# A routed feed-forward layer on one core: group 2's weights loaded later, logits' parts added on TensorE, counts by choice, tables in five parts, one subtraction moved ahead

## The chip, the cores and the metric

One core of a Trainium2 chip runs one program. The metric is the device time of one execution, in microseconds (us). The kernel before takes 1415.31 us, the median of 3 runs (1414.93 to 1415.47).

## What is computed

The reference adds to x (4 x 1024 rows of 512 floats) a mixture-of-experts layer applied to a rotated x. Cut to what matters:

```python
rot = hamilton(q_left_n, hamilton(filtered(x), q_right_conj))  # 4x4 mix of the 4 quarters of a row
logits = rot @ gate_w.T                     # 4096 tokens x 8 experts
topv, topi = top_k(softmax(logits), 2)      # first and second choice of each token
gates = topv / sum(topv)
for j in range(2):                          # place of each token in its expert's list
    mask = one_hot(topi[:, j], 8)
    loc_j = cumsum(mask) - 1 + offset       # all first choices stand before the second ones
    offset += mask.sum(0)
valid = loc < 1024                          # 1024 slots for each expert
h = relu(disp @ fc1_w.T + fc1_b)            # 8 experts, 1024 slots, 512 -> 2048
eo = h @ fc2_w + fc2_b                      # 2048 -> 512
out = x + sum_over_choices(eo[slot] * gate * valid)
```

## The kernel before

Tokens lie as 128 partitions x 32 (token = 32 p + j). The five engines run programs written out by hand, tied by semaphores, with no planner: the order of the source lines of an engine is the order of its work. There are three stages.

**Routing.** x comes in eight chunks of 4 tiles (512 tokens). For each of 32 units (chunk, quarter of the row) TensorE makes four 128x128 transposes (line 1171), ScalarE takes the high part (518), VectorE the low part (796), and TensorE, three units behind, multiplies both with the rotated gate weights, 16 columns: 8 for the high and 8 for the low part of those weights (1151, 1152). After four units ScalarE copies the 16 x 512 sums into `logitsT` (512), and `turn_logits` (1154 to 1160) turns them with four transposes into 128 x 16 pieces of a PSUM bank: seven times within the loop, and once after it. VectorE then adds the two parts into `lg` with one reduction (817), and chooses twice: `reduce_max`, equality, product, `reduce_max`, equality (821 to 825), with the first choice masked out of `score` (827) in between. `hot` holds the one-hot masks of both choices.

One scan over 512 columns counts both choices at once (831). TensorE turns the last counts of each partition into starting numbers (1188, 1189: sums over the partitions before, and for the second choice all first choices too). VectorE adds them, masks with `hot`, and reduces to a place for each token (838 to 840). Then come the tables: for each choice and half of j (JH = 16 tiles), in four parts, VectorE makes `hot_t` (861), `hot_b` (863) and `hot_q` (865), ScalarE the second half of `hot_q` (538), and TensorE multiplies the two with 16 matmuls a part (1203) into `token_ps`: the token of each slot. Line 868 subtracts the first low parts of group 0's weights before VectorE waits for these matmuls (`hots_used`); 870 to 872 make `gather_row`, by which GpSimd gathers the first eight blocks of rows (392), one indirect DMA for each. `idle` (1194) keeps TensorE busy with products that nobody reads.

**The first slab.** TensorE turns the gathered rows (1212), and VectorE rotates them (`rotate_ps` 949 to 959, 12 instructions a call; `rotate_half` 961 to 972) upon first terms that ScalarE wrote (569). TensorE makes one quarter itself (1219). VectorE's order is written out at 989 to 1007:

```python
turn_w1(1); sum_w1(1, 0); sum_w1(1, 1); sum_w1(1, 2)
rotate_ps(0)
w1_low_parts(1, 0)
rotate_ps(1); rotate_half(2)
y_low(0, B11, y11); y_low(0, B21, y21)
rotate_half(3)
```

`w1_low_parts(1, 0)` (786) makes the first low parts of group 1's weights; it waits for ScalarE's high parts (502) alone. Sums of the rotated halves follow (909, 913, 916), and TensorE goes on at 1296.

**The experts.** 8 experts, each with two slabs of 512 slots, a Strassen-like scheme of seven products for fc1 in `product` (1228 to 1230, three matmuls for a float32 product) and `fc2` (1253 to 1263). Weights of fc1 come in groups of two tiles.

**SP's queue.** It loads x, group 0's weights `load_w1(0)`, copies x to the output (309), then has `load_w1(1)`, `load_w1(2)`, `cut_x(0)` and `cut_x(1)` in this order (310 to 313). `load_w1` issues 8 DMAs of 64 KB, and waits for VectorE's transpose of the group before (286), since the buffer `w1_raw` has room for one group. `cut_x` waits for rows that GpSimd gathered and stored (298). Group 2's weights are first used by `turn_and_sum(2)` (1043), and `turn_x(0)` (1075) is the first user of `cut_x(0)`; it stands behind that line.

Of the kernel before, what the change touches and what calls it, by code (L numbers as in the profile page):

```python
# [11 lines left out]
ALU = mybir.AluOpType  # L12
# [6 lines left out]
def program(nc, x, cond, q_right, spectral, gate_w, fc1_w, fc1_b, fc2_w, fc2_b, out):  # L19
# [19 lines left out]
    JH = TJ // 2  # L39
    BLK = 32  # L40
# [35 lines left out]
    with ctx:  # L76
# [46 lines left out]
        lg = sb("lg", [P, TJ, E], where=early)  # L123
# [62 lines left out]
        logits_hl = xp_all.rearrange("p (j a e) -> p j a e", a=2, e=E)  # L186
        ahead_ps = hp[:, 0, 0:TOPK * E]
# [80 lines left out]
        def _(sp):  # L268
# [41 lines left out]
            load_w1(1)  # L310
            load_w1(2)
# [27 lines left out]
        def _(pool):  # L339
            chain = [0]  # L340

            def link(ins):
# [6 lines left out]
                               pattern=[[-1, P]], channel_multiplier=1).then_inc(consts_ready, 1)  # L349
            link(pool.memset(sign[:, :, :, :], 1.0))  # L350
# [29 lines left out]
            pool.wait_ge(counts_ready, 1)  # L380
# [112 lines left out]
        def _(act):  # L493
# [41 lines left out]
            for c in range(2 * TOPK):  # L535
                k, pairs = c // 2, slice(c % 2 * JH // 2, (c % 2 + 1) * JH // 2)
                act.wait_ge(hot_t_ready, c + 1)
                act.activation(hot_q[:, k, pairs, 1, :, :], hot_t[:, c % 2, :, :, :], ACT.Copy, scale=part_f[:, :]
                               ).then_inc(hots_p_ready, 1)
# [177 lines left out]
        def _(dve):  # L717
# [97 lines left out]
            hot3 = hot[:, :, :, :].rearrange("p k e j -> p (k e) j")  # L815
            dve.wait_ge(logits_T, CHUNKS)
            link(dve.tensor_reduce(lg[:, :, :], logits_hl.rearrange("p j a e -> p j e a"), X, ALU.add))
            first_bc = first_f[:, :].unsqueeze(1).to_broadcast([P, TJ, E])
            for k, (v, w, from_) in enumerate(((mx, w1m, lg[:, :, :]), (v2, w2m, score[:, :, :]))):
# [6 lines left out]
                if k == 0:  # L826
                    dve.scalar_tensor_tensor(score[:, :, :], hot_k, -1e30, lg[:, :, :], ALU.mult, ALU.add).then_inc(masked, 1)
                    dve.wait_ge(masked, 1)

            dve.wait_ge(consts_ready, 3)  # L830
            dve.tensor_tensor_scan(cnt[:, :, :].rearrange("p k j -> p (k j)"),
                                   carry[:, :, :].rearrange("p k j -> p (k j)"),
                                   hot[:, :, :, :].rearrange("p k e j -> p (k e j)"), 0.0, ALU.mult, ALU.add
                                   ).then_inc(counts_ready, 1)
# [14 lines left out]
            def of_pairs(ap, width):  # L849

                return ap.rearrange("p (m t) -> p m t", t=2).unsqueeze(2).to_broadcast([P, JH // 2, width, 2])

            for c in range(2 * TOPK):
                k, js = c // 2, slice(c % 2 * JH, (c % 2 + 1) * JH)
                pairs = slice(c % 2 * JH // 2, (c % 2 + 1) * JH // 2)
                numbers = value[:, :, :].unsqueeze(1).to_broadcast([P, JH // 2, P, 2])
# [3 lines left out]
                blocks = spaced[:, :, :].unsqueeze(1).to_broadcast([P, JH // 2, BLOCKS, 2])  # L860
                dve.tensor_tensor(hot_t[:, c % 2, :, :, :], blocks, of_pairs(q_f[:, k, js], BLOCKS),
                                  ALU.is_equal).then_inc(hot_t_ready, 1)
                dve.tensor_tensor(hot_b[:, k, pairs, :, :], numbers, of_pairs(b_f[:, k, js], P), ALU.is_equal)
                dve.wait_ge(hot_t_ready, c + 1)
                dve.tensor_tensor(hot_q[:, k, pairs, 0, :, :], hot_t[:, c % 2, :, :, :], of_pairs(j1[:, js], BLOCKS),
                                  ALU.mult).then_inc(hots_ready, 1)

            w1_low_parts(0, 0)
            dve.wait_ge(hots_used, 2 * TOPK)
# [122 lines left out]
            sum_w1(1, 2)  # L992
            rotate_ps(0)
            w1_low_parts(1, 0)
# [133 lines left out]
        def _(pe):  # L1128
# [70 lines left out]
            for c in range(2 * TOPK):  # L1199
                pe.wait_ge(hots_ready, c + 1)  # L1200
                pe.wait_ge(hots_p_ready, c + 1)
                for j in range(c % 2 * JH, (c % 2 + 1) * JH):
                    ins = pe.matmul(token_ps, hot_b[:, c // 2, j // 2, :, j % 2], hot_q[:, c // 2, j // 2, :, :, j % 2],
                                    start=(c == 0 and j == 0), stop=(c == 2 * TOPK - 1 and j == TJ - 1))
# [200 lines left out]
```

## Time and profile before

| what | value |
|---|---|
| median of 3 runs | 1415.31 us (1414.93 to 1415.47) |
| the profiled execution, its own time | 1415.69 us |
| span of that execution in the trace | 1413.7 us |
| TensorE busy in the span | 1378.0 us (97%) |
| VectorE / ScalarE / GpSimd busy | 1053.3 / 705.0 / 314.6 us |
| mean granted TensorE clock | 0.99 of full speed |

Engines are PE (TensorE matmul), PEld (TensorE weight load, beside PE), DVE (VectorE), ACT (ScalarE), POOL (GpSimd), SP (its DMA queue). A row of a timeline has the start in us, the time from the first start to the last end, the engine, the line, the operation with written and read tiles, shapes, and in brackets how long the engine stood idle before it and what ended that. "x4" is four instructions merged into one row. In the chain of waits each row is a step of the chain that ended last, with its start and the time that it adds. A busy engine says little by itself: what counts is the wait that ends last at each step.

### The profile page before, as it was taken

The numbers are of one execution on the slowest core, as the hardware profiler recorded it, in microseconds if no ns is written. First come the engines' busy times: TensorE is split into PE (matmuls) and PEld (weight loads), VectorE is DVE, ScalarE is ACT, GpSimd is POOL, SyncE is SP. The second block draws the span as 40 slices with busy tenths as digits, with TensorE's granted clock in tenths as the row PEclk, the third lists the DMA queues.
The fourth block names the chain that finished last, engine by engine and source line by source line (L and its number), as shares of the span: only waits on it lengthen the run. The fifth ranks groups of instructions, "written<-read, shape, count | busy, mean of one in ns | idle before, by whom it ended". The sixth has DMA issues, their size and how long they took to land.

```text
span 1413.7 us, 18054 instructions
## 1 busy us (share of the span) xinstructions
PE 1378.0 (97%) x6175; PEld 1131.0 (80%) x6175; DVE 1053.3 (75%) x1582; ACT 705.0 (50%) x1058; POOL 314.6 (22%) x333
## 2 busy tenths in 40 slices
PE   8679999999999999999999999999999999999997
PEld 6458888888888888888888888888888888888885
DVE  6898779687877778687886878687796868865443
ACT  5456455544555445455464455454455454644442
POOL 1174203320125103221034202241032200220021
PEclk9799999999999999999999999999999999999998
DMA  8677666656457555566466565575465533543232
GB/s 286 252 175 180 131 129 178 156 115 140 106 164 172 133 99 157 150 133 146 88 187 164 106 136 133 144 162 137 90 179 148 110 75 67 156 119 69 52 104 74
DMA packets 449676, 194.41 MB, mean 138 GB/s; under 512 B 398464, under 2 KB 401673, under 8 KB 447794
## 3 DMA queue, kind: packets, MB, share of 16 engines
q1 hardware_dynamic: 427378, 125.98, 40.5%
q0 software_dynamic: 22208, 67.29, 15.3%
q8 instruction: 49, 0.80, 0.2%
q14 instruction: 41, 0.34, 0.1%
HBM read 153.47 MB, written 39.98 MB: 137 GB/s over the span
## 4 chain that ended last, share of the span: by engine, by line
PE 95%; DVE 3%; DMA 1%; issue 1%; ACT 0%; SPq 0%; POOL 0%; POOLq 0%
PE ps L1253 15%; PE ps L1257 15%; PE ps L1263 15%; PE ps L1228 14%; PE ps L1229 14%; PE ps L1230 14%; PE ps L1171 1%; PE ps L1244 1%; PE ps L1245 1%; PE ps L1246 1%; DVE yfull L958 1%; PE ps L1151 1%; PE ps L1152 1%; DMA x_all<-in_x 0%; DVE yfull L971 0%
## 5 line engine op out<-in xcount | busy, mean ns | idle before, releaser
L1228 PE MATMUL ps<-yc_hi,w1c_hi 128*128 128x512 f32 x896 | 349.5, 390 | 1.2 <-DVE yc_lo L924 1.2
L1230 PE MATMUL ps<-yc_hi,w1c_lo 128*128 128x512 f32 x896 | 348.7, 389 | 0.0
L1229 PE MATMUL ps<-yc_lo,w1c_hi 128*128 128x512 f32 x896 | 348.6, 389 | 0.0
L1253 PE MATMUL ps<-w_hi,h_hi 128*128 128x512 f32 x952 | 254.4, 389 | 0.0
L1257 PE MATMUL ps<-w_hi,h_lo 128*128 128x512 f32 x952 | 254.4, 389 | 0.0
L1263 PE MATMUL ps<-w_lo,h_hi 128*128 128x512 f32 x952 | 254.4, 389 | 0.0
L1263 PEld LDWEIGHTS ps<-w_lo,h_hi 128*128 128x128 f32 x952 | 178.7, 188 | 37.2
L1253 PEld LDWEIGHTS ps<-w_hi,h_hi 128*128 128x128 f32 x952 | 178.7, 188 | 37.1
L1257 PEld LDWEIGHTS ps<-w_hi,h_lo 128*128 128x128 f32 x952 | 178.7, 188 | 37.0
L1228 PEld LDWEIGHTS ps<-yc_hi,w1c_hi 128*128 128x128 f32 x896 | 168.1, 188 | 39.2 <-DVE yc_lo L924 2.2
L1230 PEld LDWEIGHTS ps<-yc_hi,w1c_lo 128*128 128x128 f32 x896 | 168.2, 188 | 35.3
L1229 PEld LDWEIGHTS ps<-yc_lo,w1c_hi 128*128 128x128 f32 x896 | 168.2, 188 | 34.4
L897 DVE TENSOR_TENSOR w_lo<-w_raw,w_hi 128x512 fp32r<-128x512 f32 x232 | 158.3, 683 | 0.4 <-ACT w_hi L554 0.4
L891 DVE TENSOR_TENSOR w1c_lo<-w1t,w1c_hi 128x1792 fp32r<-128x1792 f32 x62 | 125.6, 2026 | 31.5 <-ACT w1c_hi L547 31.5
L692 ACT ACTIVATE h_hi<-h 128x512 fp32r<-128x512 f32 x128 | 80.9, 632 | 134.8 <-PE ps L1263 117.0
L554 ACT ACTIVATE w_hi<-w_raw 128x512 fp32r<-128x512 f32 x232 | 143.7, 620 | 0.4 <-DMA w_raw<-in_L_ffn_fc_w 0.4
L976 DVE SCALAR_TENSOR_TENSOR h_lo<-h,h_hi 128x512 fp32r<-128x512 f32 x128 | 88.4, 692 | 57.7 <-ACT h_hi L692 56.6
L547 ACT ACTIVATE w1c_hi<-w1t 128x1792 fp32r<-128x1792 f32 x62 | 105.8, 1706 | 44.7 <-DVE w1t L781 44.7
L976 DVE SCALAR_TENSOR_TENSOR h_lo<-ps,h_hi 128x512 fp32r<-128x512 f32 x64 | 44.0, 688 | 106.3 <-ACT h_hi L598 106.3
L1013 DVE SCALAR_TENSOR_TENSOR h<-ps,b1T,s 128x512 f32<-128x512 f32 x64 | 47.8, 747 | 91.2 <-PE ps L1230 91.1
L946 DVE SCALAR_TENSOR_TENSOR yfull<-x_turned,rot,yfull 128x512 f32<-128x512 f32 x168 | 114.8, 746 | 0.0
L654 ACT ACTIVATE s<-ps 128x512 f32<-128x512 f32 x64 | 38.3, 598 | 142.7 <-PE ps L1230 142.7
(182 smaller groups left out, 1506.4 us busy)
## 6 DMA issues: line engine op xcount, KB each, us to landing
w_raw<-in_L_ffn_fc_w SPq DMA_DIRECT2D x232, 256.0 KB, 3.0
w_raw<-in_L_ffn_fc_w SPq DMA_DIRECT2D x512, 64.0 KB
slots_dram<-x_blk POOLq DMA_DIRECT2D x28, 512.0 KB, 3.8
x_blk<-slots_dram SPq DMA_DIRECT2D x224, 64.0 KB, 2.6
out<-x_all SPq DMA_DIRECT2D x8, 1024.0 KB, 13.0
x_all<-in_x SPq DMA_DIRECT2D x6, 1024.0 KB, 13.7
b_bc<-in_L_ffn_fc_b POOLq DMA_DIRECT2D x8, 256.0 KB, 3.8
x_all<-in_x SPq DMA_DIRECT2D x4, 256.0 KB, 3.8
```

What stands on the lines that cost most here:

```text
L547: act.activation(w1c_hi[:, G % 2, :, :], w1t[:, 1:8, :], ACT.Copy).then_inc(w1_hi_ready, 1)
L554: act.activation(w2_hi[:, v % 3, :], w2_raw[:, v % 3, :], ACT.Copy).then_inc(w2_hi_ready, 1)
L891: dve.tensor_tensor(w1c_lo[:, G % 2, :, :], w1t[:, 1:8, :], w1c_hi[:, G % 2, :, :].bitcast(F32), ALU.subtract).then_inc(w1_ready, 1)
L897: dve.tensor_tensor(w2_lo[:, v % 3, :], w2_raw[:, v % 3, :], w2_hi[:, v % 3, :].bitcast(F32), ALU.subtract).then_inc(w2_ready, 1)
L946: ins = dve.scalar_tensor_tensor(y, x_turned[:, :, j, :], rot[:, i, j:j + 1], y, ALU.mult, ALU.add)
L976: dve.scalar_tensor_tensor(h_lo[:, N % 3, :], full, 0.0, h_hi[:, N % 3, :].bitcast(F32), ALU.max, ALU.subtract).then_inc(h_ready, 1)
L1228: pe.matmul(bank, hi, yc_hi[:, y, q, :], start=first and q == 0, stop=False, skip_group_check=True)
L1229: pe.matmul(bank, hi, yc_lo[:, y, q, :], start=False, stop=False, skip_group_check=True)
L1230: ins = pe.matmul(bank, lo, yc_hi[:, y, q, :], start=False, stop=last and q == 1, skip_group_check=True)
L1253: pe.matmul(eo_s[:, b, :], h_hi[:, c, blk], w2_hi[:, w, :], start=False, stop=False, skip_group_check=True)
L1257: pe.matmul(eo_s[:, b, :], h_lo[:, c, blk], w2_hi[:, w, :], start=False, stop=False, skip_group_check=True)
L1263: ins = pe.matmul(eo_s[:, b, :], h_hi[:, c, blk], w2_lo[:, w, :], start=False, stop=False, skip_group_check=True)
```

## The change

It makes five edits, all in the first 112 us of the program. `load_w1(2)` now waits, on SP's queue, for the eight gathers of the first slab. `turn_logits` multiplies by a 16 x 8 matrix `both_parts` (two identities, one above the other) in place of transposing, so that both parts are added on TensorE and the reduction into `lg` is gone; the choices read PSUM. The counts are scanned for each choice by itself, and TensorE's starting numbers come in two steps. The tables are made in five parts in place of four, the last two of 8 tiles. `w1_low_parts(1, 0)` stands before `rotate_ps(0)`.

```diff
+    PARTS = ((0, 0, JH), (0, JH, TJ), (1, 0, JH), (1, JH, TJ - JH // 2), (1, TJ - JH // 2, TJ))
-        lg = sb("lg", [P, TJ, E], where=early)
+        both_parts = sb("both_parts", [2 * E, E], where=early)
-        logits_hl = xp_all.rearrange("p (j a e) -> p j a e", a=2, e=E)
-        ahead_ps = hp[:, 0, 0:TOPK * E]
+        logits_ps = xp_all[:, 0:TJ * E].rearrange("p (j e) -> p j e", e=E)
+        ahead_ps = [hp[:, k, 0:E] for k in range(TOPK)]
...
             load_w1(1)
+
+            for arrived in x0_in:
+                sp.wait_ge(arrived, 16)
             load_w1(2)
...
+            pool.wait_ge(consts_ready, 1)
+            pool.tensor_tensor(both_parts[:, :], ident[0:2 * E, 0:E], ident[0:2 * E, E:2 * E], ALU.add)
...
-            pool.wait_ge(counts_ready, 1)
+            pool.wait_ge(counts_ready, 2)
...
-            for c in range(2 * TOPK):
-                k, pairs = c // 2, slice(c % 2 * JH // 2, (c % 2 + 1) * JH // 2)
+            for c, (k, begin, end) in enumerate(PARTS):
                 act.wait_ge(hot_t_ready, c + 1)
...
             dve.wait_ge(logits_T, CHUNKS)
-            link(dve.tensor_reduce(lg[:, :, :], logits_hl.rearrange("p j a e -> p j e a"), X, ALU.add))
-            for k, (v, w, from_) in enumerate(((mx, w1m, lg[:, :, :]), (v2, w2m, score[:, :, :]))):
+            for k, (v, w, from_) in enumerate(((mx, w1m, logits_ps), (v2, w2m, score[:, :, :]))):
...
-            dve.wait_ge(consts_ready, 3)
-            dve.tensor_tensor_scan(cnt[:, :, :].rearrange("p k j -> p (k j)"),
+                    dve.wait_ge(consts_ready, 3)
+                dve.tensor_tensor_scan(cnt[:, k * E:(k + 1) * E, :].rearrange("p e j -> p (e j)"),
...
-            dve.wait_ge(ahead_ready, 1)
-            link(dve.tensor_tensor(cnt[:, :, :], cnt[:, :, :], ahead_ps.unsqueeze(2).to_broadcast([P, TOPK * E, TJ]), ALU.add))
-            link(dve.tensor_tensor(loc[:, :, :], cnt[:, :, :], hot3, ALU.mult))
+            for k in range(TOPK):
+                of_k = slice(k * E, (k + 1) * E)
+                dve.wait_ge(ahead_ready, k + 1)
+                link(dve.tensor_tensor(cnt[:, of_k, :], cnt[:, of_k, :], ahead_ps[k].unsqueeze(2).to_broadcast([P, E, TJ]), ALU.add))
+                ins = dve.tensor_tensor(loc[:, of_k, :], cnt[:, of_k, :], hot[:, k, :, :], ALU.mult)
+            link(ins)
...
-            for c in range(2 * TOPK):
-                k, js = c // 2, slice(c % 2 * JH, (c % 2 + 1) * JH)
-                pairs = slice(c % 2 * JH // 2, (c % 2 + 1) * JH // 2)
+            for c, (k, begin, end) in enumerate(PARTS):
+                js, pairs, m = slice(begin, end), slice(begin // 2, end // 2), (end - begin) // 2
...
             w1_low_parts(0, 0)
-            dve.wait_ge(hots_used, 2 * TOPK)
+            dve.wait_ge(hots_used, len(PARTS))
...
             sum_w1(1, 2)
+            w1_low_parts(1, 0)
             rotate_ps(0)
-            w1_low_parts(1, 0)
             rotate_ps(1)
...
-                    at = (g * XC + t) * 2 * E
-                    ins = pe.transpose(xp_all[:, at:at + 2 * E], logitsT[:, g % 2, t * P:(t + 1) * P],
-                                       ident[0:2 * E, 0:2 * E])
+                    at = (g * XC + t) * E
+                    ins = pe.matmul(xp_all[:, at:at + E], logitsT[:, g % 2, t * P:(t + 1) * P], both_parts[:, :],
+                                    start=True, stop=True)
...
             pe.wait_ge(counts_ready, 1)
-            pe.matmul(ahead_ps, before[:, :], cnt[:, :, TJ - 1], start=True, stop=False)
-            pe.matmul(ahead_ps[:, E:2 * E], ones[:, :], cnt[:, 0:E, TJ - 1], start=False, stop=True).then_inc(ahead_ready, 1)
+            pe.matmul(ahead_ps[1], ones[:, :], cnt[:, 0:E, TJ - 1], start=True, stop=False)
+            pe.matmul(ahead_ps[0], before[:, :], cnt[:, 0:E, TJ - 1], start=True, stop=True).then_inc(ahead_ready, 1)
+            pe.wait_ge(counts_ready, 2)
+            pe.matmul(ahead_ps[1], before[:, :], cnt[:, E:2 * E, TJ - 1], start=False, stop=True).then_inc(ahead_ready, 1)
...
-            for c in range(2 * TOPK):
+            for c, (k, begin, end) in enumerate(PARTS):
                 pe.wait_ge(hots_ready, c + 1)
                 pe.wait_ge(hots_p_ready, c + 1)
-                for j in range(c % 2 * JH, (c % 2 + 1) * JH):
+                for j in range(begin, end):
```

## Rows read from the trace of the kernel before

**Rows 1.** The page's first line.

```profile
span 1413.7 us, 18054 instructions
```

**Rows 2.** The chain of waits, 26 to 31 us: start, us, what.

```profile
26.48 0.35 PE ps L1158 x4
...
30.58 0.35 PE ps L1158 x4
```

**Rows 3.** Table by stretch: stretch, length, each engine's busy us, PEclk, DMA share, GB/s.

```profile
14.00:42.00 28.00, 28.00 (x189) 19.20 (x188) 20.88 (x36) 18.69 (x34) 0.00 (x0) 1.00 0.96 339
44.00:57.00 13.00, 5.50 (x15) 4.39 (x16) 11.26 (x23) 5.43 (x14) 3.55 (x7) 0.53 1.02 380
...
66.00:68.00 2.00, 2.00 (x17) 1.90 (x16) 0.85 (x3) 0.00 (x0) 0.00 (x0) 0.50 0.00 0
```

**Rows 4.** TensorE: two rows of the timeline; line 1219's loads, ns min/median/max.

```profile
51.76 0.58 PE L1188 MATMUL ps<-cnt,before 128*128 128x16 f32 x2 [7.50 <-DVE cnt L831]
52.17 0.57 PE L1189 MATMUL ps<-cnt,ones 128*128 128x8 f32 x2
...
L1219 PEld LDWEIGHTS ps<-x_turned,rows x32: 190/190/192, 85.3 to 91.8; 128*128 128x128 f32 x32
```

**Rows 5.** Timeline of VectorE, from the logits to the places.

```profile
44.03 0.69 DVE L817 TENSOR_REDUCE lg<-ps 128x256 f32<-128x512 f32 x1 [2.06 <-PE ps L1158]
...
45.22 0.42 DVE L822 TENSOR_TENSOR s<-lg,st 128x256 f32<-128x256 f32 x1
...
50.38 1.23 DVE L831 TENSOR_TENSOR_SCAN cnt<-carry,s 128x512 f32<-128x512 f32 x1
...
52.78 0.69 DVE L838 TENSOR_TENSOR cnt<-cnt,ps 128x512 f32<-128x512 f32 x1 [1.09 <-PE ps L1189]
...
53.51 0.69 DVE L839 TENSOR_TENSOR loc<-cnt,s 128x512 f32<-128x512 f32 x1
...
54.23 1.05 DVE L840 TENSOR_REDUCE place<-loc 128x64 f32<-128x512 f32 x1
```

**Rows 6.** Timeline of the tables' last part, VectorE and TensorE.

```profile
63.20 0.68 DVE L861 TENSOR_TENSOR hot_t<-spaced,q_f 128x1024 bf16<-128x1024 bf16 x1
...
63.80 1.21 DVE L863 TENSOR_TENSOR hot_b<-value,b_f 128x2048 bf16<-128x2048 bf16 x1
...
64.93 0.68 DVE L865 TENSOR_TENSOR hot_q<-hot_t,j 128x1024 bf16<-128x1024 bf16 x1
...
65.53 0.94 DVE L786 TENSOR_TENSOR w1c_lo<-w1t,w1c_hi 128x768 fp32r<-128x768 f32 x1
65.67 1.89 PE L1203 MATMUL ps<-hot_q,hot_b 128*128 128x128 bf16 x16 [1.25 <-DVE hot_q L865]
...
67.59 0.22 DVE L870 COPY j_part<-ps 128x64 f32<-128x64 f32 x1 [1.11 <-PE ps L1203]
```

**Rows 7.** Timeline of the first gathers and the first rotations.

```profile
70.37 1.52 POOL L392 DMA_INDIRECT h<-in_x,gather_row  x1 [0.30 <-issue]
...
71.86 7.01 SPq L256 DMA_DIRECT2D w_raw<-in_L_ffn_fc_w  x8
...
72.50 0.66 PE L1212 MATMUL ps<-ident,h 128*128 128x128 f32 x4 [1.81 <-DMA h<-in_x,gather_row]
...
74.55 0.66 PE L1212 MATMUL ps<-ident,h 128*128 128x128 f32 x4 [0.71 <-DMA h<-in_x,gather_row]
...
75.75 5.05 DVE L958 SCALAR_TENSOR_TENSOR yfull<-ps,rot,yfull 128x256 f32<-128x256 f32 x12 [1.74 <-ACT yfull L569]
...
80.72 0.95 DVE L786 TENSOR_TENSOR w1c_lo<-w1t,w1c_hi 128x768 fp32r<-128x768 f32 x1
```

**Rows 8.** Timeline of SP's queue, TensorE and VectorE behind the first rotations.

```profile
89.94 14.30 SPq L256 DMA_DIRECT2D x_blk<-slots_dram  x16
...
97.94 0.93 PE L1296 MATMUL ps<-yc_hi,w1c_hi 128*128 128x512 f32 x3 [1.16 <-DVE yfull L916]
...
111.02 1.30 DVE L768 STREAM_TRANSPOSE w1t<-w_raw 128x512 f32<-128x512 f32 x2
```

More of the change, by code:

```diff
@@ L534, in _ @@
             act.wait_ge(part_ready, 1)
-            for c in range(2 * TOPK):
-                k, pairs = c // 2, slice(c % 2 * JH // 2, (c % 2 + 1) * JH // 2)
+            for c, (k, begin, end) in enumerate(PARTS):
                 act.wait_ge(hot_t_ready, c + 1)
-                act.activation(hot_q[:, k, pairs, 1, :, :], hot_t[:, c % 2, :, :, :], ACT.Copy, scale=part_f[:, :]
+                act.activation(hot_q[:, k, begin // 2:end // 2, 1, :, :], hot_t[:, c % 2, 0:(end - begin) // 2, :, :], ACT.Copy,
+                               scale=part_f[:, :]
                                ).then_inc(hots_p_ready, 1)
@@ L847, in _, with of_pairs @@
             link(dve.scalar_tensor_tensor(b_f[:, :, :], block_f[:, :, :], -float(P), place[:, :, :], ALU.mult, ALU.add))
-            def of_pairs(ap, width):
-                return ap.rearrange("p (m t) -> p m t", t=2).unsqueeze(2).to_broadcast([P, JH // 2, width, 2])
-            for c in range(2 * TOPK):
-                k, js = c // 2, slice(c % 2 * JH, (c % 2 + 1) * JH)
-                pairs = slice(c % 2 * JH // 2, (c % 2 + 1) * JH // 2)
-                numbers = value[:, :, :].unsqueeze(1).to_broadcast([P, JH // 2, P, 2])
+            for c, (k, begin, end) in enumerate(PARTS):
+                js, pairs, m = slice(begin, end), slice(begin // 2, end // 2), (end - begin) // 2
+                def of_pairs(ap, width):
+                    return ap.rearrange("p (m t) -> p m t", t=2).unsqueeze(2).to_broadcast([P, m, width, 2])
+                numbers = value[:, :, :].unsqueeze(1).to_broadcast([P, m, P, 2])
+                blocks = spaced[:, :, :].unsqueeze(1).to_broadcast([P, m, BLOCKS, 2])
+                table = hot_t[:, c % 2, 0:m, :, :]
                 if c >= 2:
@@ L859, in _ @@
                     dve.wait_ge(hots_ready, c - 1)
-                blocks = spaced[:, :, :].unsqueeze(1).to_broadcast([P, JH // 2, BLOCKS, 2])
-                dve.tensor_tensor(hot_t[:, c % 2, :, :, :], blocks, of_pairs(q_f[:, k, js], BLOCKS),
-                                  ALU.is_equal).then_inc(hot_t_ready, 1)
+                dve.tensor_tensor(table, blocks, of_pairs(q_f[:, k, js], BLOCKS), ALU.is_equal).then_inc(hot_t_ready, 1)
                 dve.tensor_tensor(hot_b[:, k, pairs, :, :], numbers, of_pairs(b_f[:, k, js], P), ALU.is_equal)
                 dve.wait_ge(hot_t_ready, c + 1)
-                dve.tensor_tensor(hot_q[:, k, pairs, 0, :, :], hot_t[:, c % 2, :, :, :], of_pairs(j1[:, js], BLOCKS),
-                                  ALU.mult).then_inc(hots_ready, 1)
+                dve.tensor_tensor(hot_q[:, k, pairs, 0, :, :], table, of_pairs(j1[:, js], BLOCKS), ALU.mult
+                                  ).then_inc(hots_ready, 1)
             w1_low_parts(0, 0)
-            dve.wait_ge(hots_used, 2 * TOPK)
+            dve.wait_ge(hots_used, len(PARTS))
             link(dve.tensor_copy(j_part[:, :], token_ps[:, 0, :]))
@@ L1198, in _ @@
             idle(12)
-            for c in range(2 * TOPK):
+            for c, (k, begin, end) in enumerate(PARTS):
                 pe.wait_ge(hots_ready, c + 1)
                 pe.wait_ge(hots_p_ready, c + 1)
-                for j in range(c % 2 * JH, (c % 2 + 1) * JH):
-                    ins = pe.matmul(token_ps, hot_b[:, c // 2, j // 2, :, j % 2], hot_q[:, c // 2, j // 2, :, :, j % 2],
-                                    start=(c == 0 and j == 0), stop=(c == 2 * TOPK - 1 and j == TJ - 1))
+                for j in range(begin, end):
+                    ins = pe.matmul(token_ps, hot_b[:, k, j // 2, :, j % 2], hot_q[:, k, j // 2, :, :, j % 2],
+                                    start=(c == 0 and j == 0), stop=(c == len(PARTS) - 1 and j == TJ - 1))
                 ins.then_inc(hots_used, 1)
```

9 lines of the change are left out of this document (4 added, 5 removed).

## The prediction

> **What bounds the kernel now.** I read the chain of waits first. The span is 1413.7 us [rows 1], and from about 110 us on every step of the chain is a TensorE matmul behind another: the experts run back to back. The change touches nothing there, so what it does to the start is passed on whole to the end. In the start the chain has four stretches.
>
> From 14 to 42 us it stays on TensorE. A turn of logits stands in it with 0.35 us for four transposes, and the next one follows 4.10 us later, like all seven of the loop [rows 2]. In the table by stretch TensorE is busy for 28.00 of 28.00 us at full clock, VectorE for 20.88 and ScalarE for 18.69 [rows 3]: there is no gap in which more TensorE work could hide. From 44 to 65.6 us VectorE holds the chain (choices, counts, tables), with one wait of 1.09 us for TensorE in between [rows 5], and a tail behind the last table [rows 6]. Then come the gathers; the second one ends VectorE's idle 1.74 us [rows 7]. From 75.75 on VectorE works without a stop until 97.8 us, where TensorE takes over after having waited 1.16 us for it [rows 8].
>
> The sum is made against the profiled execution: 1415.69 us, 2.0 over its span [rows 1], and 0.38 over the median of the runs. A difference counts for both alike.
>
> **Logits' parts on TensorE.** Four transposes become four float32 matmuls. The trace records each float32 matmul that is not a transpose as two pairs of weight load and matmul: the one instruction of line 1188 is x2, the one of 1189 too, and between their first starts lie 52.17 - 51.76 = 0.41 us, so 0.205 us a pair [rows 4]. That was at a clock of 0.53 [rows 3], nearly half speed, and neither 16 nor 8 columns mattered; so the weight load sets it, and at full clock I take 0.103 us. A turn is then 8 x 0.103 = 0.83 us, against 0.35: +0.48. Seven in the loop and one behind it, all on the chain: **+3.84**. Both ends: if the pairs follow as closely as the transposes of the same tile, 0.35 / 4 = 0.0875 us [rows 2], it is 8 x 0.35 = +2.8; if each pair pays its whole weight load of 0.190 us at full clock [rows 4], unhidden, it is 8 x (1.52 - 0.35) = +9.4. I stay with 0.103, the same kind of instruction.
>
> The Trainium skill (TensorE: Matmul & The Clock Gate, section LDWEIGHTS) says that a weight load takes its columns over 1.2 in ns, however many rows are used. For 128 columns that is an estimate of 107 ns a pair, 0.86 us a turn: +0.51 for each turn where I take +0.48, and +0.24 on the sum. The trace does not bear the rule out for transposes, which cost 87.5 ns here with 16 rows [rows 2].
>
> In return the reduction at line 817 goes, 44.03 to 44.76 with its gap: **-0.73** [rows 5]. The maximum, the equality and the masking of the first choice now read PSUM. I price that at nothing: 512 columns take 0.69 us with a PSUM operand (838) and without one (839) [rows 5]. The Trainium skill (VectorE: DVE Perf Modes, section on the TRN2 errata) charges 120 in place of 58 cycles for a PSUM source, an estimate of 0.065 us for each of three instructions, +0.19 on the sum; the same two rows speak against it.
>
> The sum of two identities on GpSimd stands before the signs, about 1.5 us into the program, over 10 us before its first reader. It costs nothing unless VectorE should come to wait for the signs, and then a few tenths at most.
>
> **Counts by choice.** The scan of 1.23 us is cut in two. A second VectorE instruction adds its fixed part: 256 columns take 0.42 and 512 take 0.69 [rows 5], so 0.15 us is fixed, of which about half overlaps the neighbour: +0.08. Behind the scan (end 51.61) the places' reduction now starts at 54.23, 2.62 us later. Afterwards TensorE has one matmul to make after the second scan, 0.58 us [rows 4] with 0.15 before and 0.04 behind, so it is ready 0.77 us after the scan. Meanwhile VectorE adds and masks the first choice: small work to +0.12, two linked instructions of 256 columns at 0.45 to +0.99; the second choice starts at about +0.93 and needs two more, so the reduction starts at +1.83. That is -0.79, with the extra scan **-0.71**. Ends: -0.4, if the first choice's work does not fit into the wait, and -0.8. Nothing else waits at `counts_ready` 2: GpSimd's next result is needed some 15 us later.
>
> **Tables in five parts.** From the rows, 1024 elements take 0.60 us of VectorE's time and 2048 take 1.13 (63.20, 63.80, 64.93): 0.53 for each 1024, 0.07 fixed [rows 6]. One part more is three instructions more, +0.21. Gained is the tail: now the last table ends at 65.61, 16 matmuls run until 67.56 at a clock of 0.50 [rows 3], and line 870 starts 1.98 us behind the table [rows 6]. With 8 matmuls left, half of 1.89, line 870 could start at 0.05 + 0.95 + 0.03 = 1.03 us behind it; VectorE's own subtraction (0.94, begun 0.08 before the end) holds it to no less than 0.89. So -0.95 + 0.21 = **-0.74**. Ends: -0.3 if the slow clock reaches the part before the last too, so that the last one queues, and -0.88 at full clock.
>
> **Group 2's loads behind the gathers.** Now they start at 71.86, in the midst of the gathers. The first gather was issued by 70.07 and had its transposes at 72.50, 2.43 us; the second by 71.89 and 74.55, 2.66 us [rows 7]. With no loads beside it I give the second the first one's time: **-0.23** (ends 0 and -0.4). The later gathers gain more, but VectorE does not wait for them. Price: SP's queue now waits for the eighth gather, about 85 us, issues 8 DMAs in 7.01 us [rows 7] until 92, and only then the cuts, which start at 89.94 and take 14.30 us now [rows 8]; they end by 106.3 in place of 104.2. Group 2's weights are first read at 111.02 [rows 8], and the cuts behind that. Both covers hold, by some 15 and at least 5 us; were the first gone, each us of lateness would cost one.
>
> **Low parts ahead.** At 80.72 the subtraction takes 0.95 us of VectorE, 0.86 of it in the chain. Placed before the rotations it starts at 74.01, where VectorE idles until 75.75 [rows 7]; it ends by 74.96, before the rotations can start (75.5). **-0.86**. End: nothing, if VectorE's chain were not the last to arrive; excluded by the 1.16 us of [rows 8].
>
> **Sum:** 3.84 - 0.73 - 0.71 - 0.74 - 0.23 - 0.86 = +0.57 us: 1415.69 becomes 1416.26, and the median 1415.31 becomes 1415.9.
>
> A measurement of this kernel can tell about 0.2% from no change, 2.8 us. Forecast: **within it**, slightly on the slow side.
>
> **Rivals.**
> *The second pairs are free* (chance 0.10). If the second pair of each matmul ran under the first's shadow, the +3.84 goes, and the rest is 0.57 - 3.84 = -3.27: 1412.0, faster by 0.23%. For it: 8 columns are next to no streaming. Against it: the even spacing of 0.205 us at lines 1188 and 1189.
>
> *Weight loads stand open* (0.12, with what else may turn slower). In the loop other matmuls cover the weight loads; small matmuls have nothing to cover them with. At 0.190 us a pair the turn is 1.52 us, the sum -3.27 + 9.4 = +6.1: 1421.4. It becomes slower than 0.2% once a pair takes over (0.35 + 6.1 / 8) / 8 = 0.14 us at full clock. For it: a load is recorded with 0.190. Against it: lines 1188 and 1189 again, whose spacing at half clock is already only 0.205.
> The Trainium skill (FP8 and Floating Point Precision, section TensorE Precision Notes) counts four passes for true float32; if each of them loaded weights, a turn would be 16 x 0.103 = 1.65 us and the time 1422.4, in this rival too, but the trace records two loads.
>
> *The moved loads bring nothing* (inside the forecast, 0.2 of its chance): the second gather's time is its own latency, and the sum is +0.80: 1416.1.
>
> **How the numbers follow.** The forecast has 0.78. Its own range: the lower ends together, 2.8 - 0.73 - 0.8 - 0.88 - 0.4 - 0.86 = -0.9; the weak ends, 3.84 - 0.73 - 0.4 - 0.3 - 0 - 0.86 = +1.55, and to +2.8 for pairs of up to 0.14 us. So 1414.4 to 1418.1. To hold 8 in 10 with both rivals aside I reach somewhat to each: 1413.4 to 1418.8. Faster 0.10, within 0.78, slower 0.12.
>
> **What would show it.** Line 1158 with two pairs for each matmul, a turn of 0.8 us in the chain, groups of units 4.6 us apart in place of 4.1, and the loop's end 3.4 us later. No `lg`. The reduction of places 1.8 us behind the second scan. The last table part 8 matmuls, line 870 about 1 us behind it. SP's loads of group 2 after 82 us, `w1c_lo` of line 786 in VectorE's idle time before the rotations, and rotations starting at once behind each other. TensorE's take-over (1296) about 0.6 us later than 97.94. Wrong it would be with a turn near 0.35 or over 1.1 us, with a loop that had slack after all, or with a stall past 106 us on group 2's weights.

## The result, and the profile after

| | kernel before | changed kernel |
|---|---|---|
| median of the runs, us | 1415.51 (1414.51 to 1417.07) | 1418.03 (1417.06 to 1421.34) |
| ratio, 95% interval | 1 | 1.0021 (1.0013 to 1.0029) |
| profiled execution, us | 1415.69 | 1417.70 |
| its span, us | 1413.7 | 1415.7 |

The change makes the kernel slower, by 2.5 us in the medians, where the prediction said 0.57. That is the edge of what it called "within 0.2%", and inside its range (1413.4 to 1418.8). A ratio of 1 lies outside the interval, so the slowdown is real, though small.

First the opening lines of the profile's page for the changed kernel; they answer to [rows 1].

```profile
span 1415.7 us, 18135 instructions
## 1 busy us (share of the span) xinstructions
PE 1384.5 (98%) x6209; PEld 1138.7 (80%) x6209; DVE 1053.1 (74%) x1587; ACT 705.8 (50%) x1059; POOL 309.9 (22%) x334
```

Next the chain of waits of the changed kernel, 16 to 31 us, against [rows 2].

```profile
16.65 0.98 PE ps L1165 x8
...
21.39 0.98 PE ps L1165 x8
...
26.13 0.98 PE ps L1165 x8
```

The four transposes with 0.35 us became eight pairs (x8: two for each of four matmuls) with 0.98 us, and a turn comes every 4.74 us in place of 4.10. So a turn costs 0.63 more where the prediction had 0.48, and a pair 0.12 us in place of 0.103. The weight loads themselves are recorded with 0.187 us (one line's instructions, line 1165), so neighbouring pairs overlap in part:

```profile
L1165 PEld LDWEIGHTS ps<-both_parts,logitsT x64: 181/187/187, 16.6 to 47.2; 16*128 16x128 f32 x64
```

VectorE's timeline of the changed kernel, from the first choice to the places, answers to [rows 5]. Line 826 is the maximum of each choice, 827 the equality behind it, 835 a scan, 844 and 845 add and mask the counts, 847 reduces to the places.

```profile
47.52 0.42 DVE L826 TENSOR_REDUCE st<-ps 128x32 f32<-128x256 f32 x1 [3.35 <-PE ps L1165]
47.98 0.42 DVE L827 TENSOR_TENSOR s<-ps,st 128x256 f32<-128x256 f32 x1
...
51.22 0.40 DVE L826 TENSOR_REDUCE st<-score 128x32 f32<-128x256 f32 x1
51.65 0.42 DVE L827 TENSOR_TENSOR s<-score,st 128x256 f32<-128x256 f32 x1
...
53.70 0.69 DVE L835 TENSOR_TENSOR_SCAN cnt<-carry,s 128x256 f32<-128x256 f32 x1
...
54.39 0.41 DVE L844 TENSOR_TENSOR cnt<-cnt,ps 128x256 f32<-128x256 f32 x1
54.83 0.44 DVE L845 TENSOR_TENSOR loc<-cnt,s 128x256 f32<-128x256 f32 x1
55.19 0.41 DVE L844 TENSOR_TENSOR cnt<-cnt,ps 128x256 f32<-128x256 f32 x1
55.63 0.46 DVE L845 TENSOR_TENSOR loc<-cnt,s 128x256 f32<-128x256 f32 x1
56.13 1.05 DVE L847 TENSOR_REDUCE place<-loc 128x64 f32<-128x512 f32 x1
```

The wait of 1.09 us for TensorE is gone. The second scan ends by 54.39, and the places' reduction begins 1.74 us later; the prediction said 1.8.

The timeline of the tables' last part, VectorE and TensorE, answers to [rows 6].

```profile
67.31 0.42 DVE L872 TENSOR_TENSOR hot_q<-hot_t,j 128x512 bf16<-128x512 bf16 x1
67.64 0.95 DVE L793 TENSOR_TENSOR w1c_lo<-w1t,w1c_hi 128x768 fp32r<-128x768 f32 x1
67.79 0.63 PE L1213 MATMUL ps<-hot_q,hot_b 128*128 128x128 bf16 x8 [0.53 <-DVE hot_q L872]
...
68.51 0.22 DVE L877 COPY j_part<-ps 128x64 f32<-128x64 f32 x1
```

Eight matmuls are left behind the last table, and line 877 (870 before) starts 0.78 us behind the table's end by the record (67.73), where it was 1.98: VectorE goes from its own subtraction into it with no wait.

Last the timeline of the gathered rows and the first rotations, against [rows 7] and [rows 8].

```profile
70.03 0.96 POOL L399 DMA_INDIRECT h<-in_x,gather_row  x1 [13.19 <-DVE gather_row L879]
73.51 1.11 PE L1222 MATMUL ps<-ident,h 128*128 128x128 f32 x4 [2.51 <-DMA h<-in_x,gather_row]
74.27 1.63 PE L1204 MATMUL ps<-w1c_hi 128*128 128x512 f32 x3
74.85 0.95 DVE L793 TENSOR_TENSOR w1c_lo<-w1t,w1c_hi 128x768 fp32r<-128x768 f32 x1
75.70 1.00 PE L1222 MATMUL ps<-ident,h 128*128 128x128 f32 x4
77.25 10.01 DVE L965 SCALAR_TENSOR_TENSOR yfull<-ps,rot,yfull 128x256 f32<-128x256 f32 x24 [1.45 <-ACT yfull L576]
87.17 2.74 DVE L978 SCALAR_TENSOR_TENSOR yfull<-x_turned,rot,yfull 128x256 f32<-128x256 f32 x6
...
83.03 5.77 SPq L258 DMA_DIRECT2D w_raw<-in_L_ffn_fc_w  x8
90.86 7.50 SPq L258 DMA_DIRECT2D x_blk<-slots_dram  x8
```

The low part now lies in VectorE's idle time, and the 24 rotations run without a break. SP's loads of group 2 start at 83.03; those weights are turned at 111.69 with no wait, so both covers held. But the transposes take 1.11 and 1.00 us where they took 0.66, and three idle matmuls 1.63 where they took 0.94. The table by stretch of the changed kernel says why (columns as in [rows 3]); the first of its rows is the loop of the logits.

```profile
14.00:48.00 34.00, 32.93 (x218) 23.64 (x215) 20.47 (x37) 19.80 (x36) 0.00 (x0) 1.00 0.98 363
...
72.00:78.00 6.00, 4.49 (x20) 3.88 (x21) 4.45 (x9) 2.10 (x5) 4.64 (x5) 0.72 0.65 176
```

From 72 to 78 us the granted clock was 0.72, with part of the stretch (73.1 to 76.5 us) at the lower of the two levels (1.2 of 2.4 GHz). It fell near the end of TensorE's wait of 2.51 us for the gathered rows; before, there was a wait as well (1.81 us), but the transposes there ran at full clock. So the second block's transposes began 5.67 us behind the first gather's issue; before it was 74.55 - 69.11 = 5.44.

### The profile page after: what moved, and what is told of

It is laid out like the page before. It is cut to its first block, busy times and chain, and to the rows that moved or that the text cites. A ratio compares the mean times of both kernels' runs of the same rounds, so it can differ in the third digit from the quotient of the medians.

```text
span 1415.7 us, 18135 instructions
## 1 busy us (share of the span) xinstructions
PE 1384.5 (98%) x6209; PEld 1138.7 (80%) x6209; DVE 1053.1 (74%) x1587; ACT 705.8 (50%) x1059; POOL 309.9 (22%) x334
## 4 chain that ended last, share of the span: by engine, by line
PE 94%; DVE 3%; DMA 1%; issue 1%; ACT 0%; SPq 0%; another core or an unknown queue 0%; POOL 0%; POOLq 0%; ACTq 0%
PE ps L1267 15%; PE ps L1263 15%; PE ps L1273 15%; PE ps L1238 14%; PE ps L1240 14%; PE ps L1239 14%; PE ps L1254 1%; PE ps L1255 1%; PE ps L1256 1%; PE ps L1178 1%; DVE yfull L965 1%; DMA x_all<-in_x 1%; PE ps L1165 1%; PE ps L1158 0%; PE ps L1159 0%
```

## The experiments

I compare executions by marks: when the same instruction starts, minus its start in the profiled execution of the kernel before (us, negative is earlier). A turn is one group of logits on TensorE, "take-over" is line 1296, "fc2" the first matmul of the second layer in group 0 (110.53 before) and in group 1 (118.69 before).

| | first turn | seventh turn | last turn | places | line 870 | rotations | take-over | fc2, group 0 | fc2, group 1 |
|---|---|---|---|---|---|---|---|---|---|
| changed kernel | -1.63 | +2.22 | +2.85 | +1.90 | +0.92 | +1.49 | +0.97 | +0.66 | +1.98 |
| e2, logits only | +0.10 | +3.95 | +4.58 | +4.50 | +4.31 | +4.66 | | +4.64 | +4.82 |
| e3, without logits | -1.43 | -0.45 | -0.44 | -1.31 | -2.04 | -1.83 | -2.43 | -2.63 | -1.20 |
| e4, longer idle | -0.09 | +3.75 | +4.39 | +3.44 | +2.46 | +2.15 | | +1.58 | +2.70 |
| e9, before again | -1.76 | +0.05 | +0.05 | +0.06 | +0.05 | -0.13 | -0.13 | -0.13 | +0.93 |
| e10, changed again | -1.73 | +2.11 | +2.75 | +1.80 | +1.17 | +1.39 | +0.88 | +0.59 | +1.65 |

**e1, the changed kernel again**, on the chip of e2 to e4.

> The changed kernel once more. In its first trace TensorE's fc2 stood 0.66 us later than before at 110.5 us, but two announcements of finished matmuls reached ScalarE 1.4 and 1.7 us late between 111 and 117 us, and the span came out 2.0 us longer. Theory A (a chance event of that execution): here no such late announcement, group 1 stays unbroken, and the profile's shift at fc2's first matmul (110.53 before) of 0.5 to 2 us is the shift at the end. Theory B (the change makes it, by what its later loads do to the DMA traffic): a wait of about 1 us before TensorE's group 1 shows again near 117 us. Time 1416.5 to 1418.5 by either; a turn of logits 0.98 us in the chain.

Measured: 1418.37 us, 1.0015 (1.0006 to 1.0024). The slowdown repeats, about 2.3 us by the medians.

**e2, the logits' edit alone**, made on the kernel before:

```diff
-                    at = (g * XC + t) * 2 * E
-                    ins = pe.transpose(xp_all[:, at:at + 2 * E], ..., ident[0:2 * E, 0:2 * E])
+                    at = (g * XC + t) * E
+                    ins = pe.matmul(xp_all[:, at:at + E], ..., both_parts[:, :], start=True, stop=True)
...
-            link(dve.tensor_reduce(lg[:, :, :], logits_hl.rearrange("p j a e -> p j e a"), X, ALU.add))
```

> The kernel before with the logits' parts added on TensorE and nothing else changed. Theory A: a turn costs 0.98 in place of 0.35 us, eight of them on the chain, +5.0, less 0.73 for the reduction: +4.3 us, 1419.8 against 1415.5. Rival (the loop has slack, the time comes from elsewhere): less than +1.5 us.

Measured: 1419.55 us, 1.0018 (1.0009 to 1.0027). The ratios given with the runs are those on record, with their intervals; they need not be the quotient of the two medians, which would be 1.0024 here. Its loop began almost where that of before did, and fc2 comes 4.64 us late: 8 x 0.63 = 5.04 for the turns, 0.73 back for the reduction, and 0.35 lost between line 870 and the rotations. The median says less than the trace: 1419.55 is 3.4 us above the 1416.12 of the kernel before that was timed beside it. e9 below shows one place where such a price can hide, but e3 shows a higher price for the same edit.

**e3, the change without the logits' edit**: the reverse of that diff, made on the changed kernel.

> The changed kernel with the four transposes and the reduction on VectorE put back; the other four edits stay. Theory A: the four edits bring -0.9 (counts) -1.0 (tables) -0.86 (low parts) and -0.2 to +0.6 (gathers, and TensorE's clock that falls before them), so -2.2 to -3.0 us against before: 1412.5 to 1413.3. Rival (the moved loads cost as much as the rest gains): within 1 us of before.

Measured: 1413.51 us, 0.998 (0.9971 to 0.9989). The other four parts together gain 2.6 us, and the logits' edit costs more than they bring: 1418.37 - 1413.51 = 4.9 us. So the same edit cost 3.4 us on the kernel before and 4.9 us on the other four parts; the price by turns, 5.04 - 0.73 = 4.3, lies between. This version beats both kernels, by 0.2%.

**e4, longer idle work**, to test whether the clock ahead of the rotations is what was lost:

```diff
-            idle(11)
+            idle(16)
```

> The changed kernel with 16 in place of 11 products that nobody reads ahead of the first gathered rows. In its trace TensorE's clock fell to 0.5 at 72.9 us, the first transposes took 1.11 in place of 0.66 us, the three idle products behind them 1.63 in place of 0.94, and the second block's transposes waited behind these. Theory A: the 5 products (1.1 us at full clock) close the idle time of 2.51 us before 73.5 far enough that the clock stays at full, and VectorE's rotations start 0.5 to 0.8 us earlier: 0.5 to 0.8 us less than e1. Rival (the gather's landing alone sets that start): no difference to e1.

Measured: 1418.61 us, 1.0019 (1.001 to 1.0028). The table by stretch and TensorE's timeline of e4:

```profile
74.00:78.00 4.00, 2.64 (x14) 1.75 (x14) 3.35 (x8) 1.45 (x3) 3.08 (x4) 1.00 0.67 176
...
74.98 0.66 PE L1222 MATMUL ps<-ident,h 128*128 128x128 f32 x4 [1.32 <-DMA h<-in_x,gather_row]
75.39 0.94 PE L1204 MATMUL ps<-w1c_hi 128*128 128x512 f32 x3
76.71 0.66 PE L1222 MATMUL ps<-ident,h 128*128 128x128 f32 x4 [0.38 <-DMA h<-in_x,gather_row]
```

TensorE waits 1.32 us in place of 2.51 for the first rows, the granted clock stays 1.00, the transposes take 0.66 again, and the rotations start 6.35 us behind the first gather's issue, against 7.22 in the changed kernel (6.86 in e1, 6.64 before). The clock did cost 0.5 us or more at this place. That is not seen in the median: 1418.61 beside e1's 1418.37 is no gain. The trace of e4 cannot settle it either, since its loop began late: the last turn stands 1.5 us behind that of the changed kernel.

**e5 to e8, one part alone on the kernel before**: counts by choice, tables in five parts, and the two moves.

```diff
-            dve.tensor_tensor_scan(cnt[:, :, :].rearrange(...), ...).then_inc(counts_ready, 1)
+                dve.tensor_tensor_scan(cnt[:, k * E:(k + 1) * E, :].rearrange(...), ...).then_inc(counts_ready, 1)
...
-            pe.matmul(ahead_ps, before[:, :], cnt[:, :, TJ - 1], start=True, stop=False)
-            pe.matmul(ahead_ps[:, E:2 * E], ones[:, :], cnt[:, 0:E, TJ - 1], start=False, stop=True).then_inc(ahead_ready, 1)
+            pe.matmul(ahead_ps[1], ones[:, :], cnt[:, 0:E, TJ - 1], start=True, stop=False)
+            pe.matmul(ahead_ps[0], before[:, :], cnt[:, 0:E, TJ - 1], start=True, stop=True).then_inc(ahead_ready, 1)
+            pe.wait_ge(counts_ready, 2)
+            pe.matmul(ahead_ps[1], before[:, :], cnt[:, E:2 * E, TJ - 1], start=False, stop=True).then_inc(ahead_ready, 1)
```

```diff
+    PARTS = ((0, 0, JH), (0, JH, TJ), (1, 0, JH), (1, JH, TJ - JH // 2), (1, TJ - JH // 2, TJ))
...
-            for c in range(2 * TOPK):
+            for c, (k, begin, end) in enumerate(PARTS):
```

```diff
             load_w1(1)
+            for arrived in x0_in:
+                sp.wait_ge(arrived, 16)
             load_w1(2)
...
+            w1_low_parts(1, 0)
             rotate_ps(0)
-            w1_low_parts(1, 0)
```

The first fence is e5, the second e6; of the third, the wait is e7 and the move of the low parts e8.

> The kernel before with the counts by choice alone. Theory A: the places' reduction starts 0.7 to 0.9 us earlier, less what GpSimd's subtraction, now beside a scan, takes from VectorE: -0.7 us. Rival (the scan for each choice costs as much as it hides): 0.

> The kernel before with the tables in five parts alone. Theory A: the last table ends 0.21 us later, the tail behind it falls from 1.98 to 0.9 or 1.05 us, so the first gather is issued 0.75 to 0.95 us earlier; if TensorE's clock falls before the first gathered rows as in the changed kernel, 0.3 to 0.6 us of it are given back: -0.3 to -0.9 us. Rival: TensorE's clock is slow in both of the last parts and the tail stays near 2 us: +0.2.

> The kernel before with group 2's loads behind the first gathers alone. Theory A: the second gather's rows come 0.2 to 0.3 us earlier and the later ones 2 to 3 us, of which VectorE's chain sees 0.2: -0.2 us, and no wait by TensorE between 110 and 120 us. Theory B (these loads, now beside gathers and cuts, make the late stretch that the changed kernel showed at 112 to 117 us): a wait of about 1 us by TensorE near 116 us, and +1 us.

> The kernel before with group 1's low parts ahead of the rotations alone. Theory A: the subtraction runs in VectorE's idle 1.74 us before the rotations, which start at 75.75 as before, and everything behind comes 0.86 us earlier: -0.86 us. Rival: it delays GpSimd's issue of the third and fourth gather by 0.6 us each, so that VectorE later waits for rows or for ScalarE: 0.

| | median us | ratio (95%) | stretch of its own, against before |
|---|---|---|---|
| e5 counts | 1414.43 | 0.9995 (0.9986 to 1.0004) | first choice to places -0.87 |
| e6 tables | 1414.61 | 1.0 (0.9991 to 1.0009) | first table to line 870: -0.64 (changed kernel -0.98) |
| e7 loads | 1415.94 | 1.0002 (0.9993 to 1.0011) | line 870 to the second block's transposes -0.26 |
| e8 low parts | 1414.41 | 0.9995 (0.9986 to 1.0004) | rotations to the second half -0.87, given back by fc2 |

No single part can be told from nothing by its timed runs: against 1415.27 for the kernel before, timed beside them, the medians are lower by 0.8 (e5), 0.7 (e6) and 0.9 us (e8) and higher by 0.7 (e7), and each interval holds 1. The marks inside the traces tell more. The low parts alone are the instructive one. VectorE's timeline of e8, and behind it two rows of TensorE's:

```profile
75.44 10.01 DVE L958 SCALAR_TENSOR_TENSOR yfull<-ps,rot,yfull 128x256 f32<-128x256 f32 x24 [0.73 <-ACT yfull L569]
85.36 2.71 DVE L971 SCALAR_TENSOR_TENSOR yfull<-x_turned,rot,yfull 128x256 f32<-128x256 f32 x6
88.98 2.36 DVE L924 TENSOR_TENSOR yc_lo<-yfull,yc_hi 128x1024 fp32r<-128x1024 f32 x2 [0.91 <-ACT yc_hi L619]
91.26 2.71 DVE L971 SCALAR_TENSOR_TENSOR yfull<-x_turned,rot,yfull 128x256 f32<-128x256 f32 x6
94.33 1.23 DVE L909 TENSOR_TENSOR x_turned<-ps,yfull 128x1024 f32<-128x1024 f32 x1 [0.37 <-PE ps L1219]
...
84.98 1.01 PE L1212 MATMUL ps<-ident,h 128*128 128x128 f32 x4 [0.27 <-DMA h<-in_x,gather_row]
85.79 8.43 PE L1219 MATMUL ps<-x_turned,rows 128*128 128x256 f32 x32
```

The rotations run back to back and are through 0.86 us sooner, and then VectorE waits 0.91 for ScalarE and 0.37 for TensorE, which have their input from the gathered rows. With group 2's loads still beside the gathers the last of those rows come no sooner than before: its transposes start at 84.98, before at 84.87. But the clock has a part in it: from 83 to 88 us the granted clock of e8 was 0.71, before 1.00. The last transposes took 1.01 us in place of 0.66, and the 32 matmuls of line 1219 8.43 in place of 7.07. So an estimate from these rows is that some 0.35 of the 0.91 us, and all of the 0.37, are the clock's, and 0.55 the rows'. In the changed kernel, where the loads are out of the way, the last transposes start at 82.93 and the same place has no such wait: 89.84 follows 87.17 + 2.74 at once.

This is one execution, and the profiled one of e8 took 1415.65 us where the median is 1414.41. That the low parts alone bring nothing is shown for this execution and not for e8's others.

**e9, the kernel before again, and e10, the changed kernel again**, on one chip, because the first profiles left two things open: seven turns cost 4.4 us and the changed kernel was only 2.85 us late at the start of the last one, since it had begun the loop 1.63 us earlier; and it lost another 1.3 us between the two fc2 marks, in group 1.

> The kernel before, profiled once more. Theory A (late announcements belong to a chip or an execution): its trace may show them, as the traces of the call with the changed kernel did and those of the single edits did not. Theory B (they belong to the change): never here. Besides, its first trace had a slow clock from 10.5 to 14.0 us; without it the loop is 1 to 1.5 us earlier, and fc2 begins near 109.3 in place of 110.53. Time 1415.5.

> The changed kernel a third time, beside the kernel before. Theory A: late announcements only if e9 has them too; without them the end is 2.2 to 2.6 us later than e9's, measured from the first turn of logits. Theory B: TensorE waits about 1 us near 117 us again. Time +2 to +3 us on before.

Measured: e9 1415.98 us, 0.9999 (0.9989 to 1.0008); e10 1418.26, 1.002 (1.0011 to 1.003). Both questions have their answer in e9. Its chain of waits, 30 to 36 us:

```profile
30.81 3.25 DMA w_raw<-in_L_ffn_fc_w
...
34.09 0.71 DVE w1t L768
34.80 0.59 DVE xT_lo L796
...
35.43 0.41 PE ps L1151
```

This execution began its loop 1.76 us earlier than the recorded one and had nothing of it left by the seventh turn: the loop stops for group 0's weights, which VectorE has to turn (TensorE waits 0.44 and 0.96 us for VectorE behind them). VectorE's timeline of e9:

```profile
30.65 0.71 DVE L768 STREAM_TRANSPOSE w1t<-w_raw 128x512 f32<-128x512 f32 x1 [1.79 <-DMA w_raw<-in_L_ffn_fc_w]
...
34.09 0.71 DVE L768 STREAM_TRANSPOSE w1t<-w_raw 128x512 f32<-128x512 f32 x1 [1.56 <-DMA w_raw<-in_L_ffn_fc_w]
```

And TensorE's and ScalarE's timelines of e9 in group 1:

```profile
116.09 0.60 ACT L654 ACTIVATE s<-ps 128x512 f32<-128x512 f32 x1 [4.38 <-PE ps L1230]
116.74 0.50 PE L1228 MATMUL ps<-yc_hi,w1c_hi 128*128 128x512 f32 x1 [0.75 <-ACT s L654]
```

The same two instructions of the changed kernel ("remote" stands where the profile found nothing on this core that ended the wait):

```profile
117.15 0.60 ACT L661 ACTIVATE s<-ps 128x512 f32<-128x512 f32 x1 [3.28 <-remote]
117.80 0.50 PE L1238 MATMUL ps<-yc_hi,w1c_hi 128*128 128x512 f32 x1 [1.00 <-ACT s L661]
```

The kernel before has the stall in group 1 too, so it isn't the change's: TensorE waits 0.75 us for it here and 1.00 in the changed kernel.

**e11, loads and low parts together** on the kernel before, and **e12, the best version with e4's idle work**: e3 and `idle(16)`.

> The kernel before with group 2's loads behind the gathers and the low parts ahead of the rotations, both. Theory A (the second needs the first: with the loads in their old place the rows for the third and fourth quarter or TensorE's own product come late): from the first turn of logits to fc2 it takes 0.9 to 1.1 us less than the kernel before, time -1.0 us. Rival (both only give TensorE more idle time, its clock falls, and the gain is gone): 0.

> The changed kernel with the transposes and the reduction back, and 16 in place of 11 idle products: e3 and e4 together. Theory A: e3's -2.6 us, and no slow clock between 66 and 100 us, which in e4 brought 0.5 us of the stretch from the first gather to the rotations: -3.0 us, 1412.5. Rival (the clock costs nothing that ends last): as e3, -2.6.

Measured: e11 1416.66 us, 1.0004 (0.9995 to 1.0013). At the start of the second half of the rotations it is 2.73 us ahead of the recorded execution, of which 0.79 came with the loop and 0.8 with a tail of the tables that ran at full clock. Line 870 to the second half is 1.15 us shorter than before. At fc2 it is still 0.53 ahead of where line 870 stood (-2.11 against -1.58), although the granted clock was 0.66 from 83 to 88 us; e8 was there 0.34 behind its own line 870 (+0.16 against -0.18). So of the 1.15 us it keeps 0.53: VectorE waits here too, 0.25 us for ScalarE and 0.33 for TensorE. Then comes the same stall in group 1, at its longest, and with it a granted clock of 0.77 from 115 to 120 us. Two rows of e11, TensorE and ScalarE:

```profile
115.56 0.60 ACT L657 ACTIVATE s<-ps 128x512 f32<-128x512 f32 x1 [5.82 <-remote]
116.21 0.50 PE L1231 MATMUL ps<-yc_hi,w1c_hi 128*128 128x512 f32 x1 [2.19 <-ACT s L657]
```

e12: 1413.38 us, 0.998 (0.9971 to 0.9989). It is 3.0 us faster than the kernel before, timed with it at 1416.36, and equal to e3 as far as this can be measured.

## Why the prediction was nearly right, point by point

**The price of a pair: the term that was mis-sized.** "At full clock I take 0.103 us" was half of the spacing between two different instructions at half clock; measured is 0.98 / 8 = 0.12. The step that failed is the halving: a pair took 0.205 us at the lower clock and 0.12 at the full one. The sum should have had 8 x 0.63 = +5.0 where it had +3.84, 1.2 us more. The bounds (0.0875 and 0.190) held. The Trainium skill (TensorE: Matmul & The Clock Gate, section LDWEIGHTS) gives for a load an estimate of 128 / 1.2 = 107 ns; the pairs took 120 ns here and the loads are recorded with 187, so it is nearer than my 103 but still below.

**"No gap in which more TensorE work could hide": failed for four of nine executions.** Nine traces have the loop with transposes. First turn to turn 7 took 23.71 to 23.77 us in five of them (the recorded one, e5, e6, e11, e12), and there the row holds. It took 24.10 in e7, 24.70 in e3, 24.97 in e8 and 25.53 in e9, where TensorE waits for the weights of group 0, which VectorE has to turn. The recorded one had its clock at the lower level from 10.5 to 14.0 us, began its loop 1.76 us later than e9, and had the weights almost in time (VectorE waits once, 0.56 us). An early start alone does not make the wait: e12 began at 16.84 and has none, e3 at 16.78 and has one. The loop with matmuls took 27.56 us. Against e9 six turns cost 2.0 us, against the five 3.8, and against the mean of the nine (24.2) 3.3. I had read a busy share of 28.00 of 28.00 as a property of the kernel, where it was one of the execution.

**The reduction and PSUM.** `lg` is gone and 0.73 us came back. Lines 826 and 827 take 0.42 us each on the logits in PSUM and 0.40 and 0.42 on `score` in SBUF. The Trainium skill (VectorE: DVE Perf Modes, section on the TRN2 errata) has 62 cycles more for a PSUM source; these four rows show at most 0.02 us.

**Counts:** -0.71 said, -0.86 measured (e5 -0.87), a little past my end of -0.8. **Tables:** -0.74 said; -0.98 in the changed kernel, -0.64 in e6, so its cost for more instructions came out as said and the tail varied. In e5 and e11 the old four parts took 0.8 us less than in the recorded execution merely because the last one ran at full clock: 10.63 us from the first table to line 870, where five parts take 10.44 (changed kernel, e1) to 10.79 (e10). So nearly all that the fifth part gains is there only when the clock is low. **Low parts:** -0.86 said, -0.87 at its place, but "VectorE's chain is the last to arrive" did not hold in the profiled execution with this part alone: e8 gives the gain back to the gathered rows and to the clock. It stays in the changed kernel, where the moved loads let the rows come sooner. **Loads:** -0.23 said, -0.26 in e7 against the recorded execution. But that stretch, line 870 to the second block's transposes, varies by itself: 6.79 to 6.96 us in six traces with the loads in their old place, and 6.65 to 6.76 in the seven with them moved, without the changed kernel's first profile, where the clock fell. The means differ by 0.16.

**Not in the sum: the clock ahead of the rotations.** From line 870 to the rotations the changed kernel needs 0.57 us more than the kernel before, e10 0.22 and e1 0.20 more. e4 shows that it is TensorE's clock: with the gap filled the stretch is 0.3 us shorter than before's, and the granted clock 1.00.

**What the parts come to.** Like with like, e9 against the three profiles of the changed kernel, all with an early first turn: at fc2 of group 0 the change costs 0.59 + 0.13 = 0.72 (e10 and e1) to 0.79, and the spans differ by 0.7 to 1.0 us. By terms, the changed kernel against e9: start +0.1, six turns +2.0 (3.8 less the 1.8 of the weights' wait), two more turns +1.3, reduction -0.7, counts -0.9, tables -1.0, line 870 to the rotations +0.75 (77.25 - 68.51 against 75.63 - 67.64; the moved loads and the clock are both in it), low parts -0.9: +0.7 of 0.79. So +0.57 is close to this pairing, and partly by luck, by misses of opposite sign: a pair that cost more, a wait that hid some of it, and a clock that took back what the moves gave. It is not close to the medians, which say 1.9 to 2.5.

**What stays open.** The medians differ by more than the traces: 2.5, 2.3 and 1.9 us in the three comparisons. Part of it is which executions were profiled. Those of the changed kernel were below the medians of their runs (1417.70, 1417.38 and 1417.40 against 1418.03, 1418.37 and 1418.26), those of the kernel before above (1415.69 against 1415.51, 1416.62 against 1415.98). The mean offsets, 0.7 and 0.4 us, make 1.1 us of it. The traces show where a part of that lies: both profiles of the kernel before reached turn 7 late, at 41.92 and 41.98 us, where the nine traces with that loop have 40.61 to 41.98 and a mean of 41.34. Against this mean the change costs 0.6 us more than against e9, an estimate across chips and not to be added to the 1.1. And the changed loop hands a late start on in full: e2 and e4 began at 18.32 and 18.12 and reached turn 7 at 45.87 and 45.68, the three profiles of the changed kernel at 44.03 to 44.14. How often its unprofiled executions begin late, or what else they lose, no trace here shows.

**The rivals.** "Second pairs are free" fell by the first row of the chain (0.98 us). "Weight loads stand open" fell in its price (0.12, not 0.19), though its sign was right. "The moved loads bring nothing" fell, by little, at the stretch above (0.16 us); of the later rows, the last are turned from 82.93 on in the changed kernel, before from 84.87.

## What to carry to other kernels

A saving of VectorE's time in one reduction was paid with TensorE time in a loop that runs eight times: compare the price per turn, times the turns, with what is saved once. Price a small matmul by its pairs of weight load and matmul (0.12 us each here), not by its few columns. Look for slack in more than one execution: a wait for a transfer stood in four of nine traces here and not in the one recorded. And a step taken off an engine's path holds only if its inputs come sooner too; here a move that gave its 0.9 us back in the one execution profiled alone kept it in the changed kernel, where the loads beside the gathers were gone.

## What the runs showed of the hardware

**Finished matmuls announced late.** In the events of the trace the signal of a finished group of matmuls normally reaches its reader 0.40 us after the last matmul's start. In nine of the fourteen profiles, the changed kernel, e1 to e4 and e9 to e12, some signals come 1.6 to 3.4 us late, one or more in each expert's 163.5 us. Mostly nobody waits; near 116 us ScalarE does, and TensorE behind it, for 0.75 us (e9) to 2.19 us (e11). The same nine have it at the first slab, for the transposes of the gathered rows. In the changed kernel the sixth block's end at 81.24, and ScalarE, which waits for them, starts at 84.73:

```profile
80.64 0.60 PE L1222 MATMUL ps<-ident,h 128*128 128x128 f32 x4
...
84.73 1.02 ACT L619 ACTIVATE x_turned<-ps 128x1024 f32<-128x1024 f32 x1 [3.78 <-PE ps L1222]
...
85.90 8.83 PE L1229 MATMUL ps<-x_turned,rows 128*128 128x256 f32 x32 [2.31 <-ACT x_turned L619]
```

In the kernel before, ScalarE started 0.70 us behind the start of that block's transposes (82.84 - 82.14). VectorE lost nothing by it here, but TensorE waited 2.31 us, and then had the lower clock from 86.8 to 90.2. e5 to e8 and the first profile of the kernel before have no late signal. It comes with kernels that hold the change and kernels that don't: all eight profiles of two chips (e1 to e4, e9 to e12) have it, and none of the four of a third (e5 to e8). So it goes with the chip, or with the hour. Its cause is not settled, and no run was made to find it.

**The clock is a matter of gaps that move.** No two traces had all their low stretches at the same places: 10.5 to 14.0, 44.7 to 58.3 and 65.2 to 68.6 us in the recorded execution of before, 73.1 to 76.5 and 86.8 to 90.2 among others in the changed kernel. They fell where TensorE had been waiting or had little to do (2.51 and 2.31 us of waiting ahead of those two), but not every such wait lowered the clock: behind 2.43 us in e11, at 70.97 us, it stayed at 1.00. What lay in a low stretch cost up to 0.8 us more (the last part of the tables, 1.89 against 1.09 us).

**Two pairs for each float32 matmul, 0.12 us a pair** with 16 rows, 128 weight columns and 8 moving ones, at full clock, against 0.0875 us for a transpose of the same tile.
